# Feed-forward gate and up products of a decoder layer: eight block products against Strassen's seven

## What is computed

```python
x = x + _L0_attn_ref(_layernorm(x), ...)
x = x + _L0_xattn_ref(_layernorm(x), ctx_1024, ctx_1024, ...)
x = x + _L0_ffn_ref(_layernorm(x), w_gate, w_up, w_down)

def _L0_ffn_ref(x, w_gate, w_up, w_down):      # weights int32, HIDDEN = 1536, DIM = 512
    gate = jnp.einsum('bsd,hd->bsh', x, wg)    # wg = w_gate / 127, and so on
    up = jnp.einsum('bsd,hd->bsh', x, wu)
    h = jax.nn.silu(gate) * up
    return jnp.einsum('bsh,dh->bsd', h, wd)
```

## Time and profile before

| | us |
|---|---|
| median of 3 runs | 1245.09 |
| the profiled execution, its own time | 1244.3 |
| its span on the core | 1242.6 |
| PE busy | 1204.5 (97%) |
| DVE busy | 561.2 (45%) |
| ACT busy | 415.6 (33%) |
| POOL busy | 240.4 (19%), next to nothing of it in the feed-forward |

### The profile page before, as it was taken

The page is one execution under the profiler, slowest core; times in us unless marked ns, Lnnn a source line. Parts: engine busy times, 40 slices in busy tenths (PEclk is TensorE's granted clock), DMA queues, the critical chain, the costliest instruction groups (busy, mean ns, idle before and its releaser), DMA issues.

```text
span 1242.6 us, 16935 instructions
## 1 busy us (share of the span) xinstructions
PE 1204.5 (97%) x6768; PEld 977.1 (79%) x6768; DVE 561.2 (45%) x1036; ACT 415.6 (33%) x746; POOL 240.4 (19%) x230
## 2 busy tenths in 40 slices
PE   5999999999989999999999999989999999999998
PEld 4877777777767888888778888877888888888887
DVE  5667675685686633323552332353343123123112
ACT  4455455454364522222542222233322112112111
POOL 1255755654774000000000000000000000000000
PEclk9899999999999999999999999999999999999999
DMA  8010110101045520011420001133301001000000
GB/s 279 9 35 9 39 57 9 70 35 52 22 150 185 192 98 26 26 34 35 169 93 26 26 26 34 55 124 110 102 27 68 1 1 68 0 0 34 1 1 34
DMA packets 46386, 73.29 MB, mean 59 GB/s; under 512 B 4336, under 2 KB 16624, under 8 KB 46320
## 3 DMA queue, kind: packets, MB, share of 16 engines
q1 hardware_dynamic: 46320, 72.37, 17.5%
HBM read 55.58 MB, written 16.78 MB: 58 GB/s over the span
## 4 chain that ended last, share of the span: by engine, by line
PE 80%; issue 6%; DVE 6%; POOL 5%; ACT 3%; DMA 1%; POOLq 0%; DVEq 0%; ACTq 0%
PE work L173 13%; PE work L175 12%; PE work L174 12%; PE score L173 11%; PE score L175 11%; PE score L174 11%; PE score L1121 2%; PE work L1650 2%; POOL xs L514 1%; PE score L1135 1%; POOL probs L495 1%; PE work L1074 1%; DVE rsum L872 1%; PE score L1139 1%; POOL ot_l L509 1%
## 5 line engine op out<-in xcount | busy, mean ns | idle before, releaser
L173 PE MATMUL score<-fxt_h,w_hl 128*128 128x512 f32 x384 | 149.6, 390 | 0.8 <-DVE fxt_l L1913 0.8
L175 PE MATMUL score<-fxt_h,w_hl 128*128 128x512 f32 x384 | 149.4, 389 | 0.0
L174 PE MATMUL score<-fxt_l,w_hl 128*128 128x512 f32 x384 | 149.4, 389 | 0.0
L1933 DVE SCALAR_TENSOR_TENSOR hid<-score,gate 128x512 f32<-128x512 f32 x48 | 33.2, 691 | 236.6 <-ACT gate L1862 236.6
L1536 DVE TENSOR_TENSOR pt_l<-work,pt_h 128x512 fp32r<-128x512 f32 x64 | 44.0, 690 | 176.9 <-ACT pt_h L1463 176.9
L1862 ACT ACTIVATE gate<-score 128x512 f32<-128x512 f32 x48 | 28.7, 598 | 265.9 <-PE score L175 265.9
L495 POOL TENSOR_TENSOR probs<-probs,band 128x544 f32<-128x544 f32 (+1 forms) x64 | 90.9, 1421 | 73.7 <-ACT probs L626 73.5
L173 PE MATMUL score<-ct_h,x_q_h 128*128 128x512 f32 x256 | 103.0, 402 | 1.6 <-DVE ct_l L1530 1.0
L173 PE MATMUL work<-cn,pt_h 128*128 128x512 f32 x256 | 101.6, 397 | 0.0
L175 PE MATMUL score<-ct_h,x_q_l 128*128 128x512 f32 x256 | 100.2, 391 | 0.0
L175 PE MATMUL work<-cn,pt_l 128*128 128x512 f32 x256 | 99.9, 390 | 0.0
...
## 6 DMA issues: line engine op xcount, KB each, us to landing
...
```

The source lines that it names most:

```text
L173: pe.matmul(out, hi_s, hi_m, start=first, stop=False)
L174: pe.matmul(out, hi_s, lo_m, start=False, stop=False)
L175: return pe.matmul(out, lo_s, hi_m, start=False, stop=last)
L1933: V.scalar_tensor_tensor(hid[:], score[:, 2 * (f % 2) + 1, :], WSCALE, gate[:, f % 2, :], ALU.mult, ALU.mult).then_inc(hid_done, 1)
```

## The change

The feed-forward now takes the tokens in two halves of 1024 and the hidden units in six pieces of 256 for each half: 12 turns `it` of one loop (`NIT`). A piece's weights (gate, m = 0; up, m = 1) form 2 x 2 blocks of 128 hidden units by 256 of width, and the tokens 2 x 2 blocks of 256 of width by 512 tokens. Instead of eight block products there are seven (`product`, j = 0 to 6), each of 2 x 3 = 6 matmuls of 128x512, over sums and differences of blocks. In the text P0 to P6 are the products of gate and Q0 to Q6 those of up.

- The token sums are made by POOL once per half (`pool_tokens`: four operations of 128x1024), then all seven blocks are turned by PE: 56 transposes per half, `FFN_TURNS` has six places now.
- The weight sums are made by POOL, four operations of 128x256 for each of 24 weight pieces. ACT first makes the staged integers floats in place, then casts the high parts; DVE takes the low parts. `w_hl` holds three pieces only, so every weight is read from DRAM, summed and split twice, once for each half.
- The products are recombined by DVE: six operations of 128x512 for each of gate and up (`dve_u2` to `dve_c21`) and one copy by ACT (`act_first`, into `m1`). P2 accumulates on P0's bank and so waits for that copy (`m1_done`).
- The low part of the hidden values moves from DVE to POOL (`pool_hidden`).
- `down` no longer accumulates over all pieces in PSUM: eight tiles of 6 matmuls per turn, each added to `fx` by DVE (`dve_add`, eight operations per turn). Turn it's eight tiles are spread over turn it+1.
- Products use six PSUM banks in a ring (`wait_bank`): a product waits until the sixth use before it has been read.
- The tokens of the first half are loaded at tile 14 of cross-attention, and their norm (`dve_x`) stands on DVE between tiles 14 and 15.

```diff
-    FFN_TURNS = (6, 8, 12, 14)
+    FFN_TURNS = (3, 5, 7, 9, 11, 13)
+            if isinstance(g, int) and g == NB * BT - 2:
+                sp.wait_ge(split_lo, len(loads))
+                sp.wait_ge(x2_stored[1], NB * BT // 4 * 16)
+                ffn.sync_x(sp)
...
-        ffn.sync_weights(sp)
+            if isinstance(g, int) and g == NB * BT - 2:
+                ffn.pool_x(pool)
+            if isinstance(g, int) and g == NB * BT - 1:
+                pool.wait_ge(sc_ready, NB * BT * SB)
+                ffn.pool_lead(pool)
...
+            if isinstance(g, int) and g == NB * BT - 2:
+                ffn.dve_x(dve)
...
+    def wait_bank(eng, key):
+
+        n = nth_use[key] - len(banks)
+        if n < 0:
+            return
+        kind, a, b, c = uses[n]
+        if kind == "x":
+            eng.wait_ge(xt_lo, 2 * NPROD * a + 2 * b + c + 1)
+        elif c:
+            eng.wait_ge(sums_done, sums_count(a, b, {1: 1, 3: 2, 4: 4, 5: 5, 6: 6}[c]))
+        elif b:
+            eng.wait_ge(hid_done, 4 * a + 1)
+        else:
+            eng.wait_ge(silu_done, 4 * a + 1)
+
...
+    def load_w(sp, n):
+        if n >= 2:
+            sp.wait_ge(w_lo, 3 * (n - 1))
+        it, m = n // 2, n % 2
+        f = 2 * P * (it % HB)
+        sp.dma_start(stage[:, m].bitcast(I32), w_v[m][:, :, f:f + 2 * P]).then_inc(w_staged[m], 16)
+
...
     def sync_lead(sp):
-        sp.dma_start(xs[:, 0], x_v[0]).then_inc(x_landed, 16)
-        sync_weights(sp, range(2))
-        sp.wait_ge(x_landed, 16)
-        sp.dma_start(xs[:, 1], x_v[1]).then_inc(x_landed, 16)
+        load_w(sp, 0)
+        load_w(sp, 1)
+        load_wd(sp, 0)
+
...
     def sync_rest(sp):
+        load_xs(sp, 0, 0)
+        load_xs(sp, 0, 1)
+        load_w(sp, 2)
+        load_w(sp, 3)
...
+    def pool_weights(pool, n):
+
+        m = n % 2
+        pool.wait_ge(w_float, n + 1)
+        if n:
+            pool.wait_ge(w_lo, 3 * n - 1)
+
...
+        PL.tensor_tensor(place(2), blk(1, 0), blk(1, 1), ALU.add).then_inc(wsum_done, 1)
+        PL.tensor_tensor(place(1), blk(0, 0), blk(1, 0), ALU.subtract).then_inc(wsum_done, 1)
+        pool.wait_ge(wsum_done, 4 * n + 1)
+        PL.tensor_tensor(place(0), place(2), blk(0, 0), ALU.subtract).then_inc(wsum_done, 1)
+        pool.wait_ge(wsum_done, 4 * n + 3)
+        PL.tensor_tensor(place(3), blk(0, 1), place(0), ALU.subtract).then_inc(wsum_done, 1)
...
+    def pool_hidden(pool, it, q):
+        pool.wait_ge(hidh_done, 4 * it + q + 1)
+        PL.tensor_tensor(hid[:, q, 1, :], g[:, q, :], hid[:, q, 0, :].bitcast(F32), ALU.subtract).then_inc(hidl_done, 1)
+
...
+    def act_weights(act, n, piece):
+        it, m = n // 2, n % 2
+        if piece == 0:
+            act.wait_ge(w_staged[m], 16 * it + 16)
+            A.copy(stage[:, m], stage[:, m].bitcast(I32)).then_inc(w_float, 1)
+            act.wait_ge(w_float, n + 1)
+            if n >= 3:
+                wait_pe(act, "p", (n - 3) // 2, (n - 3) % 2, 6)
+            A.copy(w_parts(n, 0)[0], raw_parts(m)[0]).then_inc(w_hi, 1)
+        elif piece == 1:
+            act.wait_ge(wsum_done, 4 * n + 4)
+            A.copy(w_parts(n, 0)[1], wsum[:]).then_inc(w_hi, 1)
+        else:
+            A.copy(w_parts(n, 0)[2], raw_parts(m)[1]).then_inc(w_hi, 1)
+
...
+    def act_first(act, it, m):
+
+        wait_pe(act, "p", it, m, 0)
+        if it or m:
+            act.wait_ge(sums_done, sums_count(it, m, 0) - 5)
+        A.copy(m1[:], bank(("p", it, m, 0))).then_inc(m1_done, 1)
+
+    def act_silu(act, it, q):
+        src = (bank(("p", it, 0, 2)), C22, U4, U3)[q]
+        if q == 0:
+            wait_pe(act, "p", it, 0, 2)
+        else:
+            act.wait_ge(sums_done, sums_count(it, 0, (0, 4, 5, 6)[q]))
+        if it:
+            act.wait_ge(hidl_done, 4 * (it - 1) + q + 1)
+        A.activation(g[:, q, :], src, ACT.Silu, scale=WSCALE).then_inc(silu_done, 1)
+
+    def act_hidden(act, it, q):
+        act.wait_ge(hid_done, 4 * it + q + 1)
+        if it:
+            wait_pe(act, "d", it - 1, 3 if q in (0, 3) else TH - 1)
+        A.copy(hid[:, q, 0, :], g[:, q, :]).then_inc(hidh_done, 1)
+
...
+    def act_rest(act, last_finish):
+        for it in range(NIT):
+            more = it + 1 < NIT
+            before = it == HB - 1
+            act_first(act, it, 0)
+            if it == 0:
+                last_finish()
+            if it % HB == 0:
+                act_turned(act, it // HB, NPROD - 1)
+            if more:
+                act_weights(act, 2 * it + 2, 0)
+            act_silu(act, it, 0)
...
+            act_first(act, it, 1)
+            if more:
+                act_weights(act, 2 * it + 3, 0)
+                act_weights(act, 2 * it + 3, 1)
+                act_weights(act, 2 * it + 3, 2)
+            act_hidden(act, it, 0)
+            act_down(act, it)
+            act_hidden(act, it, 1)
+            act_hidden(act, it, 2)
+            act_hidden(act, it, 3)
...
+    def dve_u2(dve, it, m):
+        wait_pe(dve, "p", it, m, 1)
+        dve.wait_ge(m1_done, 2 * it + m + 1)
+        V.tensor_tensor(U2, bank(("p", it, m, 1)), m1[:], ALU.add).then_inc(sums_done, 1)
+
+    def dve_u3(dve, it, m):
+        wait_pe(dve, "p", it, m, 3)
+        dve.wait_ge(sums_done, sums_count(it, m, 1))
+        if m:
+            dve.wait_ge(silu_done, 4 * it + 4)
+        V.tensor_tensor(U3, bank(("p", it, m, 3)), U2, ALU.add).then_inc(sums_done, 1)
+
+    def dve_u4(dve, it, m):
+        wait_pe(dve, "p", it, m, 4)
+        V.tensor_tensor(U4, bank(("p", it, m, 4)), U2, ALU.add).then_inc(sums_done, 1)
+        dve.wait_ge(sums_done, sums_count(it, m, 2))
+        V.tensor_tensor(C22, bank(("p", it, m, 4)), U3, ALU.add).then_inc(sums_done, 1)
+
+    def dve_c12(dve, it, m):
+        wait_pe(dve, "p", it, m, 5)
+        dve.wait_ge(sums_done, sums_count(it, m, 3))
+        V.tensor_tensor(U4, bank(("p", it, m, 5)), U4, ALU.add).then_inc(sums_done, 1)
+
+    def dve_c21(dve, it, m):
+        wait_pe(dve, "p", it, m, 6)
+        V.tensor_tensor(U3, U3, bank(("p", it, m, 6)), ALU.subtract).then_inc(sums_done, 1)
+
+    def dve_hidden(dve, it, q):
+        src = (bank(("p", it, 1, 2)), C22, U4, U3)[q]
+        if q == 0:
+            wait_pe(dve, "p", it, 1, 2)
+            dve.wait_ge(silu_done, 4 * it + 1)
+        else:
+            dve.wait_ge(sums_done, sums_count(it, 1, (0, 4, 5, 6)[q]))
+        V.scalar_tensor_tensor(g[:, q, :], src, WSCALE, g[:, q, :], ALU.mult, ALU.mult).then_inc(hid_done, 1)
+
...
+            dve_u4(dve, it, 1)
+            dve_hidden(dve, it, 1)
+            dve_c12(dve, it, 1)
+            dve_hidden(dve, it, 2)
+            dve_c21(dve, it, 1)
+            dve_hidden(dve, it, 3)
+            dve_down(dve, it)
+            if more:
+                dve_weights(dve, 2 * it + 3, 1)
+                dve_weights(dve, 2 * it + 3, 2)
...
+    def product(pe, it, m, j):
+        n, key = 2 * it + m, ("p", it, m, j)
+        if m == 0 and it % HB == 0:
+            pe.wait_ge(xt_lo, 2 * NPROD * (it // HB) + 2 * j + 2)
+        pe.wait_ge(w_lo, 3 * n + W_PIECE[j])
+        if j == 2:
+            pe.wait_ge(m1_done, n + 1)
+        else:
+            wait_bank(pe, key)
+        at = W_AT[j]
+        for k in range(2):
+            c = slice(P * k, P * k + P)
+            w_h, w_l, x_h, x_l = w[:, n % 3, at, 0, c], w[:, n % 3, at, 1, c], xt[:, j, 0, k, :], xt[:, j, 1, k, :]
+            first = k == 0 and j != 2
+            PE.matmul(bank(key), w_h, x_h, start=first, stop=False, skip_group_check=True)
+            PE.matmul(bank(key), w_h, x_l, start=False, stop=False, skip_group_check=True)
+            last = PE.matmul(bank(key), w_l, x_h, start=False, stop=k == 1, skip_group_check=True)
+        end(key, last)
...
+            product(pe, it, 0, 3)
+            down(pe, it - 1, 0)
+            product(pe, it, 0, 4)
+            down(pe, it - 1, 1)
+            product(pe, it, 0, 5)
...
```

More of the change, by code:

```diff
@@ new lines, in ffn_programs, with bank, wait_pe, sums_count @@
+    banks = [score[:, i, :] for i in range(4)] + [work[:, i, :] for i in range(2)]
+    W_AT = (0, 2, 1, 3, 4, 5, 6)
+    W_PIECE = (1, 2, 1, 2, 2, 2, 3)
+    def bank(key):
+        if key[0] == "p" and key[3] == 2:
+            key = key[:3] + (0,)
+        return banks[nth_use[key] % len(banks)]
+    def wait_pe(eng, *key):
+        eng.wait_ge(pe_done, nth_event[key] + 1)
+    def sums_count(it, m, n):
+        return 12 * it + 6 * m + n
+    def wait_bank(eng, key):
[11 more added lines that the diff above has]
+            eng.wait_ge(silu_done, 4 * a + 1)
@@ new lines, in down @@
+    def down(pe, it, n):
+        if it < 0:
+            return
+        t = down_order(it)[n]
+        c = slice(P * (t % ST), P * (t % ST) + P)
+        pe.wait_ge(wd_lo, it + 1)
+        pe.wait_ge(hidl_done, 4 * it + (4 if t < ST else 3))
+        if TH * it + n >= 2:
+            pe.wait_ge(acc_done, TH * it + n - 1)
+        tiles = (0, 3) if t < ST else (2, 1)
+        for f, q in enumerate(tiles):
```

(3 more changed lines are left out.)

629 lines of the change are left out of this document (377 added, 252 removed).

## The result

The changed kernel takes 1262.38 us (median of 4 runs, 1259.94 to 1263.09), the kernel before 1244.95 us (4 runs, 1243.48 to 1245.13): a ratio of 1.0139, 95% interval 1.0122 to 1.0157. The change makes the kernel 1.4% slower. 1260 us were predicted. The profiled execution's span went from 1242.6 to 1260.6 us.

A forecast was written before the change was run, and what follows sets the result against it. PE was taken to bound the kernel, so removed matmuls and added waits count fully. The -27.3 us of PE's work and the other terms summed to +15.5 us, predicting 1260 us, range 1246 to 1273.

The forecast's parts named there:

- PE's work: Feed-forward on PE: 144 fewer matmuls save 32.6 us, 48 more transposes cost 5.3 us; net -27.3 us.
- Seam: Tile 15: the norm of 1024 tokens on DVE delays the low part PE's third transposes wait for, 6.75 us.
- Start of turn 0: Turn 0's sixth product waits for the silu, behind turn 1's gate weights queued after 2 MB of tokens: 12.9 us.
- Hand-over: Between turns, P2 waits for ACT's copy of P0 behind the last hidden value: 1.4 us per turn, 14 us.
- Rival 1: At each hand-over POOL wins the port twice before DVE's hidden product: 2.7 us instead of 1.4, 1273 us; chance 0.20.
- First hand-over: First change of turn, counted together with turn 0's Q2: 1.3 us.
- statistics: Second half's statistics on DVE in turn 2 delay an addition that an output tile waits for: 1.4 us.
- turned blocks of the second half: Between turns 5 and 6, the second half's turned blocks cost 2.0 us beyond the usual hand-over.
- End: Last eight output tiles wait for a hidden part through DVE, ACT and POOL: 2.9 us.
- Clock: After two longer PE waits the granted clock falls and matmuls run slower: 3.0 us.
- Rival 3: The hand-over between turns costs nothing and the 27.3 us saving counts: 1242 us; chance 0.13.
- Rival 2: Turn 0's start: the weights land with the 2 MB still moving, -6.5 us and some clock, about 1253; chance 0.15.

The follow-up runs named there:

- the best kernel: Changed kernel plus earlier weight transfers, the seam's last order, first copy ahead of the last hidden cast, last low part on VectorE: 1226.23 us, ratio 0.9852.

## Why the prediction was right

The forecast's mechanism held: the matmuls saved are eaten by waits of TensorE. Term by term, from the profile of the changed kernel:

- **PE's work, -27.3.** Not measured by itself, but the best kernel bears it out. With -27.3 and the old idle of 2.7 and 0.75, its remaining waits (4.6 us at the end, 1.2 for x_o, 0.8 for fxt, 0.35 for fx, 0.7 and 0.3 for low parts), the 2.3 of half speed read in the changed kernel and the 0.14 that is left of each hand-over, the sum is -19.0. Its span is 18.3 us under the one before; 0.7 us are unassigned.
- **Seam, +6.75.** 6.63 against 0.64 before, so 6.0. Right in place and size. As a cost of the norm it was wrong: taken away alone, it gives nothing, since GpSimd's chain, of which the prediction reckoned 2.0 us as an addition, runs beside it and needs as long. Those 2.0 us did not appear: TensorE came to the fourth turned block at 839.17, after the 838.1 at which the forecast has its bank free, and the two delays overlap.
- **Start of turn 0, +12.9.** 14.64 us; the store took 3.78 us where 2.1 were taken from the earlier trace rows. With a store of 2.1 us other profiles show 12.6 to 12.8. The transfer was right: 10.15 us from the issue of the tokens' loads (859.48) to ScalarE's conversion (869.63), where the forecast has 10.0.
- **Hand-over, 1.4 per turn.** 1.17. The chain of 6.2 us was right, the blocking is 0.38 us (shown by holding GpSimd back) and not 0.6. Rival 1, GpSimd twice on the port, did not happen.
- **First hand-over 1.3, statistics 1.4, turned blocks of the second half 2.0.** Measured, in this order: 1.86 us of wait at 892.09, the product of 1.63 us; 0.35 at 942.83; about 1.5 (0.83 for fxt at 1052.38, 0.9 with its restart, and 0.6 beyond the usual at 1056.41).
- **End, +2.9.** 4.60: mis-sized, because the low part of the down weights (2.28 us, stretched by GpSimd) stands on VectorE behind the last hidden product and was left out of the chain. Moving it ahead of the last two hidden products does not help: it delays them by its 1.22 us, and a low part of GpSimd that takes 1.72 us beside VectorE then ends last, at 1241.71.
- **Clock, +3.0.** 6.3: 2.33 behind the seam's wait (after taking off 0.47 us that the kernel before waits for x_ot_l in that stretch), 1.7 behind turn 0's, 2.3 at the end (eleven matmuls at 0.43 in place of 0.23 us). Two waits were counted and there are three, each worth over 1.5 us.

Sum of what was measured: -27.3 - 2.7 - 0.75 + 6.0 + 14.64 + 14.4 (eleven hand-overs with their 0.24 us of restart) + 0.35 + 0.9 + 4.6 + 6.3 = 16.4, and 0.75 us by which TensorE was late before the seam already (814.70 against 813.95), for a span that grew by 18.0; 0.8 us are unassigned. The forecast had 15.5.

The sum came out nearer than its terms. Turn 0, the end and the clock were 1.7, 1.7 and 3.3 us too small; GpSimd's chain at the seam, the hand-overs with the second half's blocks (17.3 against 15.3) and the statistics were 2.0, 2.0 and 1.05 us too large. That these nearly cancel is luck. What held is where TensorE waits, for what, and the size of the three large terms.

Rival 3 (a free hand-over) is what the kernel with the last low part on VectorE nearly makes, 13.2 us lower. Rival 2 hid the 2 MB alone, for 6.5 us; the kernel with the early transfers goes further, 17.1 us lower.

The Trainium skill (SBUF — State Buffer, Who interferes with whom) says that a VectorE instruction with two inputs in SBUF and a GpSimd instruction that reads SBUF exclude each other, and that the one issued second blocks for the whole of the first. The hidden product's 1.07 against 0.69 us agrees, and so does the low part of 128x1024: 2.28 us where GpSimd was at work already, 1.22 where VectorE began first (1236.37 against 1237.18).
